# Bounded scatters, earlier gate-up products and a second batch in two halves: a kernel of attention and experts on one core

## What is computed

```python
x = x + layernorm(attn(layernorm(x), W_act, W_val, W_rec))
x = x + layernorm(ffn(layernorm(x), gate_w, experts_w1, experts_w2, shared_gate_up, shared_down))

# attn: ct = [token before, token]
z = sigmoid(relu(ct @ W_act.T))          # pairs (re, im)
z = z / cummax(abs(z), over time)
kv = associative_scan(complex_multiply, z, over time)
r = sigmoid(relu(ct @ W_rec.T))
return (kv @ W_val.T) * r ** 4

# ffn: 64 experts of width 176, the best 6 of each token
p = softmax(x @ gate_w.T); w, idx = top_k(p, 6); w = w / sum(w)
routed = sum over the 6 of w * (silu(x @ w1[e].T) @ w2[e].T)
g, u = split(x @ shared_gate_up.T)       # two parts of width 352
return routed + (silu(g) * u) @ shared_down.T
```

## Time and profile before

| | before |
|---|---|
| median of 3 runs | 321.84 us (321.76 to 323.09) |
| the profiled execution's own time | 322.0 us |
| its span in the profile | 319.9 us |
| PE busy | 254.8 us, 80% of the span |
| DVE busy | 173.7 us, 54% |
| POOL busy | 129.0 us, 40% |
| ACT busy | 106.3 us, 33% |
| data moved by DMA | 76.06 MB, mean 238 GB/s |

### The profile page before, as it was taken

One profiled execution on the slowest core, in us unless ns is written; L12 is line 12 of the kernel. 1 busy time (PEld: TensorE's weight loads), 2 busy tenths in 40 slices (PEclk: granted clock), 3 DMA queues, 4 the chain that ended last, 5 costly groups with the idle time before them and its releaser, 6 DMA issues.

```text
span 319.9 us, 4449 instructions
## 1 busy us (share of the span) xinstructions
PE 254.8 (80%) x1354; PEld 203.4 (64%) x1354; DVE 173.7 (54%) x583; ACT 106.3 (33%) x252; POOL 129.0 (40%) x166
## 2 busy tenths in 40 slices
PE   6749958580690799810898999999999999999990
PEld 6424846440540654710897999999999999984680
DVE  4349869899582268000265777644444444439375
ACT  3483641595011541100621222223444442230032
POOL 6019200007776017774155444544444444450000
PEclk9998979676596579975799999999999999999998
DMA  7999999982332813333699999953799962169812
GB/s 225 353 341 342 341 385 375 412 340 88 107 115 101 333 53 135 120 134 123 185 293 327 294 270 396 405 167 118 228 345 309 330 248 84 66 217 399 274 34 98
DMA packets 40856, 76.06 MB, mean 238 GB/s; under 512 B 4672, under 2 KB 30848, under 8 KB 40320
## 3 DMA queue, kind: packets, MB, share of 16 engines
q1 hardware_dynamic: 35264, 60.35, 56.3%
q0 software_dynamic: 5568, 15.42, 12.8%
HBM read 44.08 MB, written 31.67 MB: 237 GB/s over the span
## 4 chain that ended last, share of the span: by engine, by line
PE 57%; issue 14%; DVE 11%; another core or an unknown queue 10%; DMA 3%; ACT 3%; SPq 0%; ACTq 0%; DVEq 0%
PE bank L817 8%; PE bank L820 8%; PE bank L827 7%; PE bank L828 7%; PE bank L707 5%; PE bank L659 5%; PE bank L835 4%; PE bank L676 3%; PE bank L667 3%; DMA rows<-y_rows 3%; DVE stats L929 2%; PE bank L685 2%; PE bank L867 2%; PE bank L894 1%
## 5 line engine op out<-in xcount | busy, mean ns | idle before, releaser
L512 POOL DMA_INDIRECT y_rows<-zbuf,token_i x66 | 63.6, 964 | 72.9 <-DVE zbuf L1200 71.3
L488 POOL DMA_INDIRECT x_slots<-rows,slot_i x48 | 46.9, 977 | 65.7 <-issue 50.4
L1200 DVE COPY zbuf<-bank 128x256 f32<-128x256 f32 x66 | 28.0, 425 | 65.3 <-PE bank L828 37.7
L625 ACT ACTIVATE hT<-bank 128x128 f32<-128x128 f32 x66 | 18.3, 277 | 87.5 <-issue 67.9
L817 PE MATMUL bank<-xT,w_sb 128*128 128x128 f32 x192 | 30.3, 281 | 15.7 <-DVE xT L1191 15.7
L1191 DVE COPY xT<-bank 128x256 f32<-128x256 f32 x66 | 27.4, 415 | 25.4 <-remote 23.2
L817 PEld LDWEIGHTS bank<-xT,w_sb 128*128 128x128 f32 x192 | 26.1, 197 | 16.0 <-issue 15.9
L827 PE MATMUL bank<-w_sb,hT 128*128 128x256 f32 x96 | 28.8, 382 | 1.4 <-ACT hT_r L626 1.4
L820 PE MATMUL bank<-xT,w_sb 128*112 128x128 f32 x192 | 29.6, 278 | 0.0
L828 PE MATMUL bank<-w_sb,hT_r 112*128 112x256 f32 x96 | 28.7, 379 | 0.0
L820 PEld LDWEIGHTS bank<-xT,w_sb 128*112 128x112 f32 x192 | 25.2, 183 | 0.0
(11 more groups left out here) (201 smaller groups left out, 448.7 us busy)
## 6 DMA issues: line engine op xcount, KB each, us to landing
w_sb<-pairs SPq DMA_DIRECT2D x24, 752.0 KB
x_slots<-hidT SPq DMA_DIRECT2D x8, 1056.0 KB, 13.1
early<-x_slots SPq DMA_DIRECT2D x64, 132.0 KB
y_rows<-zeros SPq DMA_DIRECT2D x6, 1024.0 KB, 10.8
rows<-pairs SPq DMA_DIRECT2D x8, 752.0 KB, 6.5
rows<-y_rows SPq DMA_DIRECT2D x4, 1024.0 KB, 8.4
rows<-y_rows SPq DMA_DIRECT2D x4, 512.0 KB, 7.3
y_rows<-zbuf,token_i POOLq DMA_INDIRECT x66
```

The source lines that it names most:

```text
L488: pool.indirect_dma_start(x_slots, bass.IndirectOffsetOnAxis(ap=slot_i[:, c, k:k + 1], axis=0), xrow[b][:, j, k, :], None).then_inc(sent[k ...
L512: pool.indirect_dma_start(y_rows, bass.IndirectOffsetOnAxis(ap=token_i[:, s % 16:s % 16 + 1].bitcast(U32), axis=0), yS[:, s % 8, :], None) ...
L1200: dve.tensor_copy(yS[:, s % 8, :], y_b[s % 2][:, 0:C]).then_inc(y_done, 1)
```

## The change

There are three edits. First, POOL's scatters wait: from the third of a run on, each waits until the scatter two places ahead of it has landed, with two semaphores for each run or value of k, used in turn. Second, `gate_up(1)` moves on PE from behind the value products of batch 1 to ahead of them, and waits for a new semaphore `scan_mid` that DVE gives after `scan_blocks(1)`. Third, batch 1 goes from the residual to the scatters in two units of two tiles: `UNIT` lists tiles 0 to 3, 4 and 5, and 6 and 7, and transposes, logits, ranks, `choose`, `place`, `copy_rows` and `send` go by unit. On DVE the residual of the two halves is written interleaved. The 48 scatters are the same in number and size.

```diff
+        UNIT = (range(0, TB), range(TB, TB + 2), range(TB + 2, NT))
...
-            sp.wait_ge(sent_first, 16 * TOPK * TB)
+            for p in range(2):
+                sp.wait_ge(sent_first[0][p], 16 * TOPK * TB // 2)
             for q in range(RING, RING + 4):
                 load_pair(q)
 
+            for p in range(2):
+                sp.wait_ge(sent_first[1][p], 16 * TOPK)
             for s in range(8):
                 if s < TOPK:
-                    sp.wait_ge(sent[TOPK - 1 - s], 16 * TB)
+                    for p in range(2):
+                        sp.wait_ge(sent[TOPK - 1 - s][p], 16)
                 load_rows(s)
...
-            def send(b):
-
-                pool.wait_ge(slot_done, b + 1)
-                pool.wait_ge(copies_done, TB * b + TB)
-                for k in range(TOPK)[::-1]:
-                    for j in range(TB):
-                        c = TB * b + j
-                        pool.indirect_dma_start(x_slots, bass.IndirectOffsetOnAxis(
-                            ap=slot_i[:, c, k:k + 1], axis=0), xrow[b][:, j, k, :], None).then_inc(sent[k] if b else sent_first, 16)
+            def send(u):
+
+                pool.wait_ge(slot_done, u + 1)
+                pool.wait_ge(copies_done, UNIT[u][-1] + 1)
+                wide = len(UNIT[u])
+                for n in range(TOPK * wide):
+                    k, c = TOPK - 1 - n // wide, UNIT[u][n % wide]
+                    if n >= 2 and u < 2:
+                        pool.wait_ge(sent_first[u][n % 2], 16 * (n // 2))
+                    if n >= 2 and u == 2:
+                        pool.wait_ge(sent[k + 1][n % 2], 16)
+                    pool.indirect_dma_start(x_slots, bass.IndirectOffsetOnAxis(
+                        ap=slot_i[:, c, k:k + 1], axis=0), xrow[c // TB][:, c % TB, k, :], None
+                        ).then_inc(sent_first[u][n % 2] if u < 2 else sent[k][n % 2], 16)
...
             send(1)
+            send(2)
...
-            for b in range(B):
-                first_rsqrt(2 + 2 * b, TB * b)
...
+            first_rsqrt(6, 6, 2)
+            turned(1)
+            normalise(6, in_work, in_work, 6, first=1, n=2)
+            first_rsqrt(7, 6, 2)
+            normalise(7, in_row, in_x, 6, first=1, n=2)
+            copy_rows(1)
+            turned(2)
             gate_silu(1)
+            copy_rows(2)
             gate_silu(2)
-            copy_rows(1)
             gate_silu(3)
...
+            pe.wait_ge(scan_mid, 1)
+            pe.wait_ge(r_th, 4)
+            gate_up(1)
             pe.wait_ge(kv_done, 2)
             pe.wait_ge(z_th, 4)
             product_v(2)
             product_v(3)
-            pe.wait_ge(r_th, 4)
-            gate_up(1)
             gate_up(2)
...
             gate_up(0)
-            residual(1)
+            gated(2)
+            dve.wait_ge(y_mul, 3)
+            stats_of(in_work, (4, 5))
+            variances(4, 2)
+            gated(3)
...
+            choose(1)
+            columns(2)
+            place(1)
             gate_up(1)
-            choose(1)
+            choose(2)
+            place(2)
             gate_up(2)
-            place(1)
```

More of the change, by code:

```diff
@@ L185, in moe_block @@
         kv_done = sem("kv_done")
+        scan_mid = sem("scan_mid")
         r_ps = sem("r_ps")
@@ L208, in moe_block @@
         init_done = sem("init_done")
-        sent_first = sem("sent_first")
-        sent = [sem(f"sent{k}") for k in range(TOPK)]
+        sent_first = [[sem(f"sent_first{u}_{p}") for p in range(2)] for u in range(2)]
+        sent = [[sem(f"sent{k}_{p}") for p in range(2)] for k in range(TOPK)]
         token_done = sem("token_done")
@@ L653, in turn, with turn_unit @@
                     yield mm
+            def turn_unit(u):
+                first, b = UNIT[u][0], UNIT[u][0] // TB
+                for k in range(KC):
+                    for c in UNIT[u]:
+                        mm = pe.transpose(x2T_b[b][k][:, P * (c % TB):P * (c % TB) + P], in_row(c)[:, P * k:P * k + P],
+                                          ident[:])
+                    mm.then_inc(x2T_ps, 1)
             def product_z(b):
@@ L679, in product_v, with logits @@
                 mm.then_inc(v_ps, 1)
-            def logits(b):
-                for c in range(TB * b, TB * b + TB):
+            def logits(u):
+                for c in UNIT[u]:
                     for k in range(KC):
@@ L789, in _ @@
             logits(1)
-            gate_up(3, (0,))
+            pe.wait_ge(norm_dve, 12)
+            pe.wait_ge(norm_act, 12)
+            turn_unit(2)
             pe.wait_ge(rank_read, 1)
             rank(1)
+            pe.wait_ge(x2T_dve, 3)
+            pe.wait_ge(x2T_act, 3)
+            logits(2)
+            gate_up(3, (0,))
+            pe.wait_ge(rank_read, 2)
+            rank(2)
             gate_up(3, (1,))
@@ L950, in sharpen, with normalise @@
                                          ).then_inc(shift_done, 1)
-            def normalise(q, dst, src, c0):
-                for c in (c0, c0 + 1):
+            def normalise(q, dst, src, c0, n=2):
+                for c in range(c0, c0 + n):
                     dve.tensor_scalar(dst(c), src(c), mv[:, c, 0:1], rstd[:, c:c + 1],
@@ L1031, in choose @@
             def choose(h):
-                cs = range(TB * h, TB * h + TB)
-                at = slice(cs.start, cs.stop)
+                cs = UNIT[h]
+                at = slice(cs[0], cs[-1] + 1)
                 dve.wait_ge(lg_ps, h + 1)
```

111 lines of the change are left out of this document (73 added, 38 removed).

## The result

The two kernels were timed on one chip (which one is not on record), four runs each:

| | before | after |
|---|---|---|
| median | 322.37 us (321.76 to 323.09) | 311.51 us (310.85 to 312.84) |
| ratio, with its 95% interval | | 0.967 (0.963 to 0.971) |
| the profiled execution's own time | 322.0 us | 310.85 us |
| its span | 319.9 us | 309.1 us |
| start of PE's `hidden` of slot 5 | 163.78 | 152.21 |

A forecast was written before the change was run, and what follows sets the result against it. Bound: POOL's row of 48 scatters with its 15.3 us gap, then the experts on PE. 322.0 - 19.6 (earlier slot 5) + 1.0 (cold start) + 1.6 (output scatters) = 305.0 us; range 298 to 316 for 8 in 10.

The forecast's parts named there:

- loads hold the scatters: Rival: a scatter of `send(1)` stands behind all four weight loads, adding 6.3 us, 311.3 us in all; chance 0.10.
- Where the gain is made: From dispatch to experts: POOL's row of scatters bounds the start, and slot 5 starts at 144.2 instead of 163.78, -19.6 us.
- backlog of eight to ten output scatters: Behind `send(2)`, piled-up output and overflow scatters without flow control cost 0 to 5 us more, taken as +1.6.
- Products at full clock: On PE, the value products of batch 1 take about 3.2 us instead of 6.38, mostly under POOL's cover.
- The slot numbers: Those of tiles 4 and 5 come at 103 to 105, so POOL's 15.3 us wait goes, all but 0 to 1.
- The spacing: On POOL, scatters with two under way start 1.375 us apart, 0.1 us more than before.
- The loads: Four pairs of weights loaded beside `send(1)` delay its scatters by 2 us, bounded by nothing and 8.3 us.
- Behind the last scatter: From the last scatter's start at 139.0 to slot 5 on PE it takes 5.2 us, giving 144.2.
- The cold start: PE, waiting ahead of each of five slots, may fall to 0.50 of the clock: +1.0 us, lower end 0.
- Late signals: PE's signals to DVE and ACT come on time; rivals had them late, 313.3 us (chance 0.17) or 325 us (0.08).

The follow-up runs named there:

- e3: The changed kernel without the waits between scatters, on chip 10: 297.10 us, ratio 0.975 to the kernel before.
- e8: The changed kernel itself, unchanged, timed on chip 4: 309.02 us, ratio 1.012 to the kernel before.
- e11: The changed kernel with the four pairs of weight loads moved into the loop of the experts, on chip 4: 310.47 us, ratio 1.013 to the kernel before.
- e2: The kernel before plus flow control of the scatters and the early `gate_up(1)`, batch 1 in one piece, on chip 10: 313.09 us, ratio 1.027.
- e4: The changed kernel with the four pairs of weight loads moved into the loop of the experts, on chip 10: 308.66 us, ratio 1.013 to the kernel before.
- e1: The kernel before plus flow control of the scatters alone, batch 1 in one run of 24, on chip 10: 315.04 us, ratio 1.035.
- e6: The changed kernel without the waits between scatters, on chip 3: 328.39 us, ratio 1.019 to the kernel before.
- e5: The changed kernel itself, unchanged, timed again on chip 3: 311.52 us, ratio 0.968 to the kernel before.
- e10: The kernel before plus flow control of the scatters alone, batch 1 in one run of 24, on chip 4: 314.26 us, ratio 1.028.
- e12: The changed kernel with three scatters under way and the four pairs of weight loads spread out, on chip 3: 314.92 us, ratio 0.977 to the kernel before.
- e9: The changed kernel with three scatters under way instead of two, on chip 4: 301.46 us, ratio 0.984 to the kernel before.

## Why the prediction was right in its sign and range, and where it was off

311.5 us lies within the range, 298 to 316, but above the 301 to 310 that the terms of the forecast allowed. It hits the rival "loads hold the scatters" (311.3) in the number, and that is luck: no scatter stood behind all four loads, and only 3.5 of the 7.0 us by which slot 5 was missed are loads. Measured on the profiled executions the sum is -11.6 + 0.8 = -10.8 us, where I had -18.6 + 1.6.

- **Where the gain is made: right.** The bound was POOL's row with its gap, and the experts behind it. PE was ready at 131.3, as said (129.9); slot 5 decides, and the rest of the span moved by 0.8 us. I had put 1.6 us there for a backlog of eight to ten output scatters behind `send(2)`. There was none: one stood ready at 146.47. The run of five up to 160 us cost PE 1.50 us at 162.64, as before (1.43), so the 0.8 us are not accounted for.
- **Products at full clock: right.** 3.72 us for 3.2, with the granted clock at 1.00 from 83 to 86.5 us, so the gain is 2.7 of the 3.2 us. That most of it lies under POOL's cover was right as well: e3 shows the runs joined, with 0.28 us ahead of `send(1)`.
- **The slot numbers: 1.7 us late.** I had POOL start `send(1)` at 105.4; it was 107.11. About 1.0 us is the spacing in `send(0)`. The rest, 0.7 us, is the signal for `place(1)`, 5.69 us of waiting on DVE, which comes in at 105.44. On chip 4 the same step is at 101.94, and `send(1)` starts at 106.11, 1.72 us behind the start of the last scatter of `send(0)` and not 2.56.
- **The spacing: off by 0.04 us a scatter.** 1.417 and not 1.375 us, 1.0 us in each of the two rows. POOL's idle times take turns, 0.30 and 0.46 us.
- **The loads: the term that was mis-sized most.** I took 2 us; it is 145.21 - 107.11 - 23 x 1.417 = 5.5 us, and 5.9 in e8 (some 0.8 of the 5.5 is a stop at 128.81, when the loads had ended). Loading late takes 6.9 us off (e11 against e8). The step that failed is that I costed the share of bandwidth and not the landing. The scatter of 107.11 takes 6.31 us to land and the next to be waited for 4.55, against 2.45 before. With two under way, POOL starts one for each half of that. In e3, where POOL doesn't wait, landings beside the loads take 5.6 us in the median and don't stop POOL, since it waits for none of them. It was flow control that turned a slow landing into a stop.
- **The Trainium skill** (DMA: Bandwidth & Descriptors, section "Queues, rings and completion order") says that a DMA engine goes round its queues packet by packet. The trace agrees in that no scatter stood behind all four loads: that of 107.11 had landed at 113.4, and the loads kept the engines busy to about 118. But from 104 to 120 us a packet of the loads holds 5.3 KB (3.08 MB in 576) and one of the scatters 2.8 KB (0.81 MB in 288). So taking turns by packets is not an even share of bytes, which is what I had made of it. Nor does it explain the landing. If a scatter gets a third of the bytes, which is 124 of the 372 GB/s moved from 109 to 113 us, its 135 KB take 1.1 us and not 0.4. That estimate makes it land 0.7 us later, and the first landed 3.9 us later. What delays it is not shown.
- **Behind the last scatter: 1.8 us too few, and not for late signals.** From the start of the last scatter to slot 5 it is 7.0 us. I had 5.2, read from the earlier trace rows off slot 0, whose rows had been turned long before. Kernels without any late signal take as long or longer: 6.9 to 7.2 us in e2 to e4 and e8 to e11, and 8.2 in e1. The rows of slot 5 are turned 4.75 us behind the scatter, and PE turns rows one slot ahead, so `hidden` of slot 4, an output and the rows of slot 6 come before `hidden` of slot 5: 2.25 us more. In e8, where PE waits for these rows (PE's timeline):

```profile
149.29 0.44 PE L879 MATMUL bank<-ident,early 128*128 128x128 f32 x2 [0.47 <-DMA early<-x_slots]
...
151.54 0.61 PE L861 MATMUL bank<-xT,w_sb 128*128 128x128 f32 x4
```

- **The cold start: there, but free.** `hidden` of slots 0 and 1 ran at 0.50 of the clock (1.06 and 1.01 us), but the rows of slots 0 to 5 were turned 4.7 to 4.9 us behind their scatters, cold or not. The +1.0 us was nothing.
- **Late signals: not gone, only short.** I had put none into the forecast, and said that a right one would show no "remote" wait of DVE ahead of its first row copy. There is one, the 5.69 us at `place(1)`, and it cost 0.7 us. The 3.22 us at 148.54 moved slot 5 by 0.1 us at most, going by e8.

From the forecast's slot 5 (144.2, and 1.0 for the cold start) to 152.2 it is then: start of `send(1)` 1.7, spacing in the second row 1.0, loads 3.5, behind the last scatter 1.8, less the 1.0 for the cold start: 7.0 us.

**Which edit does it.** On the chip with late signals flow control is worth 16.9 us given the other two edits (e6 less e5), and these without it cost 5.1 us (e6 against the kernel before). On chips without them it is the other way round: the two edits give 8.0 us (e3), and flow control takes 9.9 or 8.8 us alone (e1, e10), and 3.6 hundredths of the ratio with the others (1.012 on chip 4 against 0.975 on chip 10), an estimated 11 us across two chips. I had named late signals as the condition, but not that they might be a matter of the chip: a profile of the kernel before from one chip cannot say that.

**What stays open.** What withholds the signals, and why it is seen on one of the three chips named here and not on two, no trace shows. Only chip 3 was used in more than one set, so whether it is the chip or something else that differed between the sets is not told apart. Whether it is POOL's issuing or the third scatter under way that brings them back is not told apart by e12, since both came together. Flow control alone, and e9 as it is, were not run on a chip with late signals. A version that is best everywhere was not found: the changed kernel is the fastest on chip 3, e3 on chip 10, and three under way gain on either kind (0.984 as e9, 0.977 as e12), though less than the best for each.

## What to carry to other kernels

Where a chain has a long piece that it puts down to no engine, look up which queue was busy without a break beside it, and test on more than one chip before the cure is built in: here flow control was worth 16.9 us on one, with the other edits, and on two others cost 9 to 10 us alone and some 11 with them. A wait on landing costs not the landing at rest but the landing beside whatever else runs then, divided by how many are under way; take its price from a stretch with the same traffic. And transfers that are moved out of the way of one engine's work must be followed to where they go: moving the loads into the expert loop freed 6 us ahead of it and lost as much or more in it.

## What the runs showed of the hardware that I had not expected

- One kernel took 5.9% more on one chip than on two others without any difference in its code: 323.3 us on chip 3 (again 323.2 in a later set), 305.1 and 305.5 on chips 10 and 4. Where both were profiled, with the kernel of e3 and e6 (297.1 and 328.4 us), the difference in the traces is late signals between engines beside rows of indirect scatters: waits of 11 to 14 us in e6, none in e3. In the profile of the kernel before that stands ahead of the change, DVE's copy of rows comes 15 us behind PE's product.
- On chip 3, with two under way, POOL pauses about 0.15 us more at every second scatter, and the waits for late signals are 1.0 to 5.1 us (e5) and not 11 to 14 (e6); in `send(0)` of e12 the limit of three never makes POOL wait, and the wait is 11.79 us again.
- A scatter of 135 KB lands in 2.3 to 2.5 us alone, and in 4.6 to 6.3 us beside loads of 752 KB that keep the DMA engines at 0.99.
